# Adjacency pieces of up to six source chunks in three places, instead of five chunks in four places

## What is computed

```python
h = relu(layernorm(x)); x = x + L0(h)   # edge weights from an MLP, weighted segment_sum(msg, dst)
h = relu(layernorm(x)); x = x + L1(h)   # two graph convolutions, 128->256->128
h = relu(layernorm(x)); x = x + L2(h)   # MLP message, segment_sum(m[src], dst), MLP update
h = relu(layernorm(x)); x = x + L3(h)   # three graph convolutions 128->128
# gcn: out = segment_sum(h[src] * norm, dst) + b
```

## Time and profile before

| | us |
|---|---|
| median of 3 runs | 4262.63 (4259.69 to 4265.24) |
| profiled execution | 4269.07 |
| its span, first to last instruction | 4267.3 |
| TensorE busy | 3218.4 (75%) |
| VectorE busy | 2219.3 (52%) |
| ScalarE busy | 1973.3 (46%) |
| GpSimd busy | 2238.3 (52%) |
| mean granted TensorE clock, share of full | 0.804 |

### The profile page before, as it was taken

One profiled execution on the slowest core, in us unless ns is written; L12 is line 12 of the kernel. 1 busy time (PEld: TensorE's weight loads), 2 busy tenths in 40 slices (PEclk: granted clock), 3 DMA queues, 4 the chain that ended last, 5 costly groups with the idle time before them and its releaser, 6 DMA issues.

```text
span 4267.3 us, 68479 instructions
## 1 busy us (share of the span) xinstructions
PE 3218.4 (75%) x19874; PEld 2621.2 (61%) x19874; DVE 2219.3 (52%) x9829; ACT 1973.3 (46%) x2929; POOL 2238.3 (52%) x1830
## 2 busy tenths in 40 slices
PE   4666667644454466676899419998999999999999
PEld 3455555433333355565687317887777788888888
DVE  6766666544444599998211001266444444444444
ACT  2222222211111255555899419964444455555555
POOL 3777777777777888888888888811000000000000
PEclk6555555555555599998999759999999999999999
DMA  4899997444444599995999549964776788888897
GB/s 132 287 310 310 302 314 220 109 109 106 100 107 108 131 233 235 232 235 118 222 240 264 112 64 255 260 193 151 218 221 205 218 264 255 252 263 253 273 295 245
DMA packets 874024, 898.42 MB, mean 211 GB/s; under 512 B 186010, under 2 KB 807169, under 8 KB 873664
## 3 DMA queue, kind: packets, MB, share of 16 engines
q1 hardware_dynamic: 700656, 785.25, 59.4%
q0 software_dynamic: 168464, 107.01, 15.4%
q10 hardware_dynamic: 4544, 1.77, 0.2%
HBM read 699.91 MB, written 193.86 MB: 209 GB/s over the span
## 4 chain that ended last, share of the span: by engine, by line
PE 40%; POOL 30%; issue 13%; DVE 12%; DMA 4%; ACT 1%; SPq 0%; DVEq 0%; POOLq 0%; ACTq 0%
PE ps L1191 27%; POOL adj L792 22%; POOL rows L784 8%; PE ps L1096 5%; PE ps L1078 3%; DMA adj<-scattering 3%; DVE same L1456 2%; DVE pre L1492 1%; DMA pieces<-adj 1%; DVE scaled L1496 1%; DVE wide L1808 1%; PE ps L1259 1%; PE ps L1264 1%; ACT wide L977 1%; PE ps L1187 1%
## 5 line engine op out<-in xcount | busy, mean ns | idle before, releaser
L1191 PE MATMUL ps<-wide,tab 128*128 128x512 f32 (+2 forms) x7644 | 1730.1, 383 | 50.7 <-DVE wide L1808 42.1
L1191 PEld LDWEIGHTS ps<-wide,tab 128*128 128x128 f32 x7644 | 1373.7, 189 | 355.4 <-DVE wide L1808 63.0
L977 ACT CAST wide<-pieces 128x1536 fp32r<-128x1536 f16 (+5 forms) x1026 | 1245.8, 1258 | 743.6 <-PE ps L1191 553.5
L792 POOL DMA_INDIRECT adj<-scattering x832 | 1310.1, 1575 | 253.7 <-issue 243.7
L784 POOL DMA_INDIRECT rows<-table,src_of x880 | 843.6, 959 | 319.3 <-issue 260.0
L1808 DVE CAST wide<-pieces 128x1024 fp32r<-128x1024 f16 (+3 forms) x604 | 397.0, 663 | 577.0 <-PE ps L1191 573.8
L1096 PE MATMUL ps<-dst_mlp,onehot_t 128*128 x2640 | 364.5, 232 | 142.1 <-DVE pre L1492 92.5
L824 POOL DMA_DIRECT2D out<-scattering x13 | 9.8, 754 | 838.3 <-DVE scattering L1773 838.3
L1096 PEld LDWEIGHTS ps<-dst_mlp,onehot_t 128*128 128x128 bf16 x2640 | 274.9, 104 | 221.8 <-issue 163.5
L1456 DVE SCALAR_TENSOR_TENSOR same<-ps,key,first_weight 128x128 bf16<-128x128 f32 x832 | 284.9, 344 | 228.3 <-PE ps L1078 227.9
L908 ACT ACTIVATE onehot<-plain,norm 128x128 f32<-128x128 bf16 x880 | 280.9, 390 | 227.0 <-DVE norm L1562 227.0
(11 more groups left out here) (262 smaller groups left out, 3542.1 us busy)
## 6 DMA issues: line engine op xcount, KB each, us to landing
pieces<-adj SPq DMA_DIRECT2D x550, 640.0 KB, 5.3
pieces<-adj SPq DMA_DIRECT2D x121, 512.0 KB, 4.8
h_rows<-rows SPq DMA_DIRECT2D x220, 256.0 KB
rows<-h_rows SPq DMA_DIRECT2D x220, 256.0 KB
onehot_list<-onehot_b SPq DMA_DIRECT2D x220, 128.0 KB, 2.8
low_row<-low_list SPq DMA_DIRECT2D x220, 128.0 KB
plain<-onehot_list SPq DMA_DIRECT2D x220, 128.0 KB
pieces<-adj SPq DMA_DIRECT2D x54, 480.0 KB, 4.6
```

What stands on the lines that cost most here:

```text
L792: nc.gpsimd.indirect_dma_start(out=adj[:, :], out_offset=bass.IndirectOffsetOnAxis(ap=place[:, k:k + 1], axis=0), in_=count16[:, k:k + 1], ...
L977: nc.scalar.copy(to, of).then_inc(cast_act, 1)
L1191: last = nc.tensor.matmul(ps_sum[SUMMED[u] % 2][:, 0:b * P], tab[q % 2][:, c, half, :], of, start=(c == u0 and half == 0), stop=(kind == " ...
```

## The change

Pieces of a four-block unit hold up to six chunks instead of five, in three places instead of four. `cut` now makes nine pieces of 49 chunks: 5, 5, 6, 5, 6, 5, 6, 5, 6. A piece of six is split 3 + 3. `PIECE_SIZE` and the number of place semaphores follow from the two constants. And VectorE no longer takes the subs of two chunks, but the second sub of each piece, of two or three chunks. ScalarE takes the first. The spare units are cut and shared as before, but their pieces use the three places too.

```diff
-PIECE_C = 5
+PIECE_C = 6
 PIECE_SIZE = PIECE_C * WIDE * P
-AR = 4
+AR = 3
...
-BY_DVE = [u >= LAST_SET and UNITS[u][4] in ("whole", "spare") and (c0 // SUB in (1, 3, 5) if UNITS[u][4] == "spare" else c1 - c0 == 2)
-          for u, c0, c1, n in SUBS]
+BY_DVE = [u >= LAST_SET and UNITS[u][4] in ("whole", "spare") and (c0 // SUB in (1, 3, 5) if UNITS[u][4] == "spare" else t > 0 and SUBS[t - 1][3] == n)
+          for t, (u, c0, c1, n) in enumerate(SUBS)]
```

## The result

| | median us (lowest to highest, runs) | ratio to before, 95% interval |
|---|---|---|
| before, beside it | 4261.16 (4259.38 to 4265.24, 4) | |
| with the change | 4328.09 (4321.21 to 4338.73, 4) | 1.0159 [1.014, 1.0178] |

The change makes the kernel 67 us slower. The forecast was 4304, so the direction held and the time lies in the range, but some 25 us of the loss were not in the sum. The profiled execution took 4327.85 us, its span 4326.0.

A forecast was written before the change was run, and what follows sets the result against it. TensorE was taken as the bound, with transfers nearly hidden and only VectorE's lateness to win. Terms of 5.8, 4.4, 6.6, 8.8, 6.6 and 9, plus 2, less 1, made +42 us: 4304, range 4271 to 4344.

The forecast's parts named there:

- The cast of three chunks: VectorE's cast of 1536 columns takes 0.956 us, on the line through the 512 and 1024 column casts.
- The update layer: Casts b5 and b6 1.12 and 1.84 us late, costing 4.4 us; a late piece 0.6 per unit, 6.6 us.
- Three places in layers 3 to 5: Less time for pieces to land: 0.3 us per unit in layers 3 and 4 (6.6), 0.8 in layer 5 (8.8).
- the longer cast's term: Layers 3 and 4: cast b3 0.26 us later per unit, 5.8 us over 22 units.
- The early pieces of four chunks: Set-by-set stage: 31 units or halves of units lose 0.3 us per piece, 9 us (2 to 13).
- The discount for fewer transfers under way: Early set-by-set pieces of 512 KB should land sooner than 4.8 us; at 4.3 a piece takes 2.15 us.
- the set-by-set stage: Early pieces of four chunks cost 9 us; fewer, longer casts save ScalarE under 1 us.
- units of three and two blocks: These units have shorter pieces for TensorE too; 2 us added to the sum.
- That three places don't sustain the rate: Rival, chance 0.15: pieces land after 6.4 us, layers 3 to 5 lose 0.19 per piece, 56 us, time 4345.
- Nothing that tells: Rival, chance 0.08: pieces of 768 KB land like those of 640; only +8 us, 4270.
- Faster: Rival, chance 0.07: fewer VectorE casts let its steps end before the next cast; up to 43 us, half gives 4241.
- the prediction's dear end for the cast: Upper end for VectorE's cast of 1536 columns: 1.39 us, in proportion to 768 columns in 693 ns.

The follow-up runs named there:

- the fourth place: The changed kernel with a fourth place of six chunks from layer 3's third unit on, in memory used otherwise before; 4306.91 us, ratio 1.0102.
- the spacing: VectorE's steps after a unit two subs apart instead of one in layers 2 to 5; 4229.8 us in the kernel before, 4313.63 in the changed one.
- the last experiment: The kernel before with VectorE's steps two subs apart in layers 2 to 5 and ScalarE's square root ahead of a cast; 4218.37 us, ratio 0.9896.

## Why the prediction was right, and where it fell short

**The cast of three chunks** was priced at 0.956 us and takes 0.960. In layers 3 and 4 it costs 0.27 us per unit (with the fourth place, where nothing else is left) against the 0.26 forecast. Right.

**The update layer** was forecast as 1.12, 1.84 and 0.6 late, and the rows show 1.2, 1.8 and 0.73; the eleven units are 12.1 us longer against 4.4 + 6.6 = 11.0. Right, step by step in these rows. No run takes the two terms apart: three places for pieces of five, with VectorE's casts and steps as before, lose 11.9 us in the same row.

**Three places in layers 3 to 5.** Layer 5 lost 0.92 us per unit against 0.8. Layers 3 and 4 lost 0.31 and 0.11 to the places (after less the fourth place) against 0.3. The sum added this to the longer cast's term, and the two in part use the same time: both layers' ten units lost 9.5 us together, against 12.4 in the sum. The step that 768 KB land in about 5.9 us holds: 5.7 now. The rise from 640 KB is 0.9 us, more than the 0.6 of the working, because pieces of 640 KB land in 4.8 instead of 5.3. Fewer places alone do not explain that, as the first of these rows shows, from the run with three places for pieces of five (line 723, from 2700 us on); the other two are from the run with the fourth place, from 3450 us on, where the rise is 0.4:

```profile
pieces<-adj SPq DMA_DIRECT2D x414, 640.0 KB, 5.2
...
pieces<-adj SPq DMA_DIRECT2D x112, 640.0 KB, 5.5
pieces<-adj SPq DMA_DIRECT2D x90, 768.0 KB, 5.9
```

So the landing time here does not follow from the size alone, and why the pieces of 640 KB came sooner is open. The Trainium skill's fit in "DMA: Bandwidth & Descriptors", section "Anatomy of one DMA — SWDGE (gpsimd) path", for transfers that GpSimd issues, gives an estimate of 0.3. On SyncE's queue the rows of the run with the fourth place (0.4) come near it, and those of the changed kernel (0.9) do not.

**The early pieces of four chunks** lost 11.2 us in 31 pieces, 0.36 each, against 0.3. The discount for fewer transfers under way was wrong for them: from 2624 to 2756 us pieces of 512 KB still take 4.7 us:

```profile
pieces<-adj SPq DMA_DIRECT2D x29, 512.0 KB, 4.7
```

The plain count, (4.7 + 2.0 + 0.1) / 3 - 1.9 = 0.37, would have been right.

**Mis-sized: the set-by-set stage.** The sum had 9 us for it, less 1 for ScalarE, and it lost 27.4. The sum priced only the early pieces. The stretches with spares 51 to 54 and the units behind them lost 5.1, 4.7 and 6.4 us more. By the starts of their units, 7.1 of these 16 lie in the four spare units, 7.3 in the whole units and 1.8 in the longer early ones. That the places are the cause the table shows: with three places for pieces of five the five rows lose 34 us, with VectorE's new share alone nothing. Three pieces per spare block took back 7.7 in their trace, 5.6 of it in the spare units. How much of the rest pieces of six have in it was not told apart by a run. ScalarE is busy for 236 of 250 us there, so a late piece finds little slack; that could have been read ahead. The last set's first piece was asked for 17.6 us later, not 8, and 26.5 us later if each trace is counted from the end of its wait for the scatter (2540.3 and 2531.4 us).

**Mis-sized: units of three and two blocks.** Forecast 2 us, measured 9.2 in layers 3 to 5. A three-block unit gives TensorE three quarters of the work per piece, but its piece of 576 KB takes 4.7 us to land against 5.7. The fourth place brings it back in full, so the cause is the places.

These two terms make 19 + 7 = 26 us, the whole gap between +42 and +67.

**The rivals.** That three places don't sustain the rate: layer 5 lost 0.10 us per piece, not 0.19, since pieces land in 5.7 and 4.8 us, not 6.4 on average. Nothing that tells: out by the time. Faster: its condition was that b3 no longer stands behind the steps. The change doesn't do that; the spacing does, and there the 43 us that the rival counted up are about what the last experiment gained, 44.

## What to carry to other kernels

With a ring of buffers, count the work between a place coming free and its next use, (places - 1) pieces less the cast, against the landing time, and do it for every kind of unit, the short ones and those with more pieces than places first: that is where the landing shrinks less than the work. Bigger pieces did not pay here for the place that was given up: a ninth more work per piece (5.44 chunks instead of 4.9) won back a third of what the fourth place is worth. And when one engine does both the next stage's input and the last stage's follow-up in one queue, spread the follow-up between the inputs before resizing buffers, and let a small instruction that another engine waits for go ahead of a long one.

## What was not expected of the hardware

VectorE's casts do not go by columns alone. By the rows above and the earlier trace rows four blocks of three chunks (1536 columns) take 0.960 us and four blocks of two (1024) 0.697, but three blocks of three (1152 columns, 16 casts) take 0.965, and three blocks of two (768) 0.693 before the change: with three blocks a cast takes as long as with four. So the prediction's dear end for the cast, 1.39, read from the row of three blocks, was no bound for four.

```profile
L1808 DVE CAST wide<-pieces 128x1152 fp32r<-128x1152 f16 x16 | 15.4, 965 | 18.9 <-PE ps L1191 12.2 <-DMA pieces<-adj 6.6
```
